# An explicit table for the side work of a Mamba and mixture-of-experts kernel

## The chip, the cores and the metric

The kernel runs on one core of a Trainium2 chip. The metric is device time in microseconds (us) of one launch, the median of several runs. Lower is better.

## The reference

The input `x` is 8 sequences of 512 tokens with 512 features, float32. Per sequence:

```
xz = W_in x ; x, z = halves (1024 channels each)
u  = silu(causal 4-tap convolution of x)
dt, B, C = W_x u (32 + 16 + 16 columns) ; delta = softplus(W_dt dt + b)
h_t = h_{t-1} * exp(delta_t * A) + delta_t * B_t * u_t      (1024 channels x 16 states)
y_t = sum over states of h_t * C_t, + D * u_t, times silu(z_t)
x1 = layernorm(x + W_out y)
out = layernorm(x1 + sum over the top 2 of 8 experts of weight * (E x1 + bias))
```

## The kernel before

**Main work.** Channels stand in 8 blocks of 128 partitions, and there are 16 states, so the recurrence of a sequence is 16 x 8 = 128 tiles of 128 x 512. The source calls each a row, numbered 0 to 127: row r is state r // 8 of block r % 8. Every row takes:

- ScalarE (ACT): `dA = exp(delta * A)`, L1384, into one of two PSUM buffers, so it waits for the scan two rows back;
- GpSimd (POOL): `dbu = u * B`, L1479, into one of four buffers, so it waits for the scan four rows back;
- VectorE (DVE): the scan `hst <- dA, dbu`, L1683.

Every second row TensorE (PE) transposes one block of 128 time steps of a finished state (8 transposes, L1053, called a part below) into `hTp`, and DVE adds it to `y` with weight C (L1511), one even row later. The sums of the last state of a sequence fall into rows 2 to 8 of the next one. SyncE (SP) issues nearly all DMAs, in one queue; at every eighth row it loads the next state's row of B, after the `dbu` of the row before.

**Side work.** All else is cut into pieces that are put between the rows of the main work, engine by engine. A piece has a name and a number, and on each engine where it has work it stands behind one row. An engine works through its rows in order: first the row's main instruction, then the row's pieces, each with its own semaphore waits. A piece whose wait is not over holds up all that stands behind it on that engine. While sequence b is scanned, the pieces do the experts' last four tiles and the output of b-2, the output projection, first layernorm, routing and experts of b-1, and the input projection, convolution and delta of b+1. Names that the text uses:

- `sz`: SP loads half a tile of silu(z) into `spare`; `gy`: POOL multiplies it into y (L1458); `yT`: PE transposes it, ACT copies it; `out`: PE multiplies by W_out (L1039, 8 shares), which `load_Wo` loads in two DMAs of 1 MB into `delta`;
- `load_res`, `load_hx`: SP loads the residual (4 DMAs) and the next sequence (1 MB, `hidT`);
- `xsL`, `moeL` (experts of tiles 11 to 14 of b-2) and `xsT`, `moe` (tiles 0 to 10 of b-1): PE transposes a tile of sorted tokens in `zs` (L1087) and multiplies by its expert's matrix (4 shares, L1039). The SP piece `xsL.k` waits until tile k is transposed and then loads tile k+2; the SP piece `moe.k` loads a later expert (1 MB) and stores the result;
- `x`: input projection, copied by ACT (L1261), three taps on DVE (L1540); `sig`, `sig2`: its silu on ACT (L1272 to L1279) and POOL (L1438); `scale`, `scatter`: ACT scales routed tokens, POOL scatters them (L1417);
- `skip`, `yinit` (PE L1071, ACT L1286), `dt`, `dt2`: D * u and delta of the next sequence; POOL ends each `dt` with two products (L1464, L1467);
- `fin`, `gather0`, `gather1`, `est`, `ln2`, `store`: the end of b-2.

**What sets the order.** `plan` (from L131 on) is a list scheduler in Python: it plays the five engines forward in steps of 0.1 us with the costs, waits and delays that `tasks` writes down for each piece, and takes, per engine, the most urgent piece that may start. `by_urgency` sorts the pieces by the length of the chain behind them plus a constant per group. `Segment` turns the result into `rows[engine][row]`, and derives from PE's order which PSUM bank and which half of `hTp` each piece uses. There are six segments: `SEG_FIRST` (head, no scan), `SEG_PRO` (sequence 0), `SEG_TWO` (1), `SEG_FULL` (2 to 6, the same table five times), `SEG_EPI` (7, whose rows are half tiles, 256 of them, scanned at L1691) and `SEG_LAST` (tail, no scan).

POOL's loop, shortened, shows how a piece stands behind a row:

```python
for step, pieces in w.rows("pool"):
    ...
    pool.wait_ge(scan_done, w.b * (NS * ND) + (n * ND + j - 3))
    nc.gpsimd.tensor_tensor(dbu[j % 4][:, :], u[w.odd][:, j, :], Bbc[n % 2][:, :], ALU.mult).then_inc(dbu_done, 1)
    ...
    for x in pieces:
        piece(w, x)
```

Of the kernel before, what the change touches and what calls it, by code (L numbers as in the profile page):

```python
# [49 lines left out]
def each(name, n):  # L50
    return [(name, j) for j in range(n)]


def per_tile(*names):
    return [(name, t) for t in range(NT) for name in names]


END = [x for g in range(0, NT, 2) for name in ("fin", "gather0", "gather1", "est", "ln2", "store") for x in ((name, g), (name, g + 1))]
MIX = [("load_Wo",)] + each("load_res", NT) + [x for t in range(NT) for x in (("sz", 2 * t), ("sz", 2 * t + 1), ("gy", 2 * t), ("gy", 2 * t + 1),
                                                                             ("yT", 2 * t), ("yT", 2 * t + 1), ("out", t))] \  # L60
    + per_tile("ln1") + each("x1T", NT) + [("gate",), ("count",), ("place",), ("route",)] + each("scale", TOP * NT) + each("scatter", TOP * NT)
def tokens(*tiles):
    return [x for k in tiles + (None,) for x in [("xsT", k)] * (k is not None) + [("moe", k - 1 if k is not None else tiles[-1])] * (k != tiles[0])]


LATE = TILES - 4
ROUTED = [("load_E",), ("load_T",), ("wT",)] + each("bias", NT) + [("load_E2",)]
MOE, MOE_EARLY = ROUTED + tokens(*range(TILES)), ROUTED + tokens(*range(LATE))
MOE_LATE = [({"xsT": "xsL", "moe": "moeL"}[x[0]], x[1]) for x in tokens(*range(LATE, TILES))]
Z = [x for i in range(HALF * NT) for x in (("z", i), ("z2", i))]  # L70
ZB = [x for i in range(HALF * NT) for x in (("zb", i), ("zb2", i))]
PRO = [("load_hx",), ("load_Wx",)] + each("x", ND) + [x for j in range(ND) for x in (("sig", j), ("sig2", j))] + [("load_wx",), ("xproj",), ("Ct",)] + each("skip", ND) + each("yinit", ND) + [x for j in range(ND) for x in (("dt", j), ("dt2", j))]


def den_tasks(x, mm):

    if x[0] != "den":
        return []
    t, e = LAST_DEN[x[1]]
    of_tile = [i for i, (u, _) in enumerate(LAST_DEN) if u == t and i < x[1]]  # L80
    late = [(("x1T", t), "act", 0.1), (("logits", NT - 1), "pe", 0)] if t >= PAIR else []
    return [("pe", mm, late + [(("load_D", e), "sp", 8 + 4 * e)] * (e in GONE)), ("dve", 0.7, [(x, "pe", 0.1), (("route", 1 if t >= PAIR else 0), "dve", 0)] + [(("den", i), "dve", 0) for i in of_tile[-1:]])]
# [7 lines left out]
def tasks(x, alone):  # L90


    name, k = x[0], x[-1] if len(x) > 1 else 0
    t = k // HALF if name in ("yT", "gy", "sz") else None
    mm, turn = 0.88, 0.6
    ev = "dve" if alone else "act"

    def silu(name, before_pe, before_act):

        if x[0] != name:  # L100
            return []
# [1645 lines left out]
```

## Time and profile before

| | |
|---|---|
| median of 3 runs | 2356.74 us (2356.3 to 2357.43) |
| profiled execution | 2358.6 us, first to last instruction |
| head, before the first scan | 72.9 us |
| sequence 0, 1, 2 | 240.6, 264.5, 277.2 us |
| sequences 3 to 6 | 272.6, 272.3, 273.9, 272.7 us |
| sequence 7 | 285.8 us |
| tail, after the last scan | 126.1 us |
| busy | DVE 89%, PE 89%, POOL 76%, ACT 64% |

The span is the only time that the profile gives for its execution; it is 1.9 us over the median of the runs. Sequence b begins with the start of its first scan: 578.0, 855.2, 1127.8, 1400.1 and 1674.0 us for b = 2 to 6. A row of the trace that gives idle time names in brackets how long the engine stood still before the instruction, and what ended that.

### The profile page before, as it was taken

What the parts mean: (1) busy time and instruction counts of PE and PEld (TensorE: products, weight loads), DVE (VectorE), ACT (ScalarE), POOL (GpSimd) and SP (SyncE); (2) the same over time, 40 slices, a digit from 0 to 9 for tenths busy, and PEclk for the clock granted to TensorE, in tenths of its full rate; (3) what the DMA queues carried; (4) which work ended last, traced back from release to release, by engine and by line L of the source; (5) the groups of instructions that cost most, each with busy time, mean ns of one, the idle gap of its engine ahead of it and who ended that gap; (6) DMA issues with size and microseconds to landing.
All of it is one profiled execution on the core that took longest, in us unless ns stands there. A gap on an engine that the chain in (4) does not pass through costs nothing.

```text
span 2358.6 us, 30155 instructions
## 1 busy us (share of the span) xinstructions
PE 2107.4 (89%) x8604; PEld 1220.5 (52%) x8604; DVE 2105.3 (89%) x2376; ACT 1516.0 (64%) x2742; POOL 1802.3 (76%) x1448
## 2 busy tenths in 40 slices
PE   9896779897989989899898998889898998889998
PEld 3344555555555555545554555455555455555543
DVE  5799999999999899999999999999999997899832
ACT  5747855785577666778566774778566785565411
POOL 2959996788887888879887889878888796685402
PEclk8896789898998999999999999999999998779999
DMA  5312031357544574446752576445743467475523
GB/s 172 108 34 74 19 139 50 128 177 258 152 109 143 179 274 132 126 148 223 255 126 93 174 266 210 112 148 201 268 125 108 154 224 255 113 246 176 185 75 84
DMA packets 205314, 367.93 MB, mean 156 GB/s; under 512 B 28472, under 2 KB 34744, under 8 KB 205152
## 3 DMA queue, kind: packets, MB, share of 16 engines
q1 hardware_dynamic: 190496, 335.60, 42.4%
q0 software_dynamic: 12544, 29.37, 5.8%
q8 instruction: 71, 1.16, 0.2%
q10 hardware_dynamic: 2112, 1.05, 0.2%
q14 instruction: 91, 0.75, 0.1%
HBM read 287.05 MB, written 78.91 MB: 155 GB/s over the span
## 4 chain that ended last, share of the span: by engine, by line
PE 29%; DVE 25%; POOL 24%; issue 12%; DMA 5%; ACT 4%; SPq 1%; DVEq 0%; POOLq 0%; ACTq 0%
PE bank L1039 20%; POOL dbu L1479 14%; DVE hst L1683 10%; DVE y L1511 6%; PE hTp L1053 6%; DVE hst L1691 3%; POOL u L1467 3%; DVE u L1540 2%; POOL delta L1464 2%; DMA zs<-sorted_tokens 2%; DMA ysb<-sorted_results,place 1%; POOL dbu L1487 1%; POOL sorted_tokens L1417 1%; ACT dA L1384 1%; PE bank L1172 1%
## 5 line engine op out<-in xcount | busy, mean ns | idle before, releaser
L1479 POOL TENSOR_TENSOR dbu<-u,Bbc 128x512 f32<-128x512 f32 x896 | 1144.6, 1313 | 210.2 <-DVE hst L1683 202.5
L1683 DVE TENSOR_TENSOR_SCAN hst<-dA,dbu 128x512 f32<-128x512 f32 x896 | 1051.8, 1205 | 17.8 <-ACT dA L1384 13.3
L1384 ACT ACTIVATE dA<-delta,negA 128x512 f32<-128x512 f32 (+1 forms) x1152 | 723.1, 639 | 457.7 <-DVE hst L1683 367.0
L1511 DVE SCALAR_TENSOR_TENSOR y<-hTp,Ct,y 128x1024 f32<-128x1024 f32 x512 | 646.2, 1262 | 47.3 <-PE hTp L1053 47.1
L1053 PEld LDWEIGHTS hTp<-ident,hst 128*128 128x128 f32 x4096 | 504.3, 151 | 354.2 <-issue 145.4
L1053 PE MATMUL hTp<-ident,hst 128*128 128x128 f32 x4096 | 574.9, 293 | 125.3 <-DVE hst L1683 34.7
L1039 PE MATMUL bank<-wslot,hidT 128*128 128x512 f32 x512 | 246.1, 616 | 21.9 <-ACT zs L1328 15.2
L1039 PE MATMUL bank<-delta,tokT 128*128 128x512 f32 x480 | 224.6, 604 | 1.5 <-issue 0.8
L1487 POOL TENSOR_TENSOR dbu<-u,Bbc 128x512 f32<-128x512 f32 x128 | 163.0, 1307 | 81.9 <-DVE hst L1691 65.4
L1039 PE MATMUL bank<-wslot,tokT 128*128 128x512 f32 x464 | 219.9, 604 | 2.6 <-ACT tokT L1343 2.1
L1039 PE MATMUL bank<-hidT,wslot 128*128 128x512 f32 x384 | 189.9, 640 | 10.0 <-DVE u L1540 7.7
L1540 DVE SCALAR_TENSOR_TENSOR u<-bank,cw,u 128x511 f32<-128x511 f32 (+2 forms) x192 | 142.1, 743 | 35.2 <-ACT u L1261 30.6
L1039 PEld LDWEIGHTS bank<-wslot,hidT 128*128 128x128 f32 x512 | 93.5, 196 | 114.5 <-issue 91.1
L1432 POOL DMA_INDIRECT ysb<-sorted_results,place x52 | 81.4, 1565 | 86.1 <-DMA ysb<-x_scratch 76.8
L1039 PEld LDWEIGHTS bank<-delta,tokT 128*128 128x128 f32 x480 | 87.3, 196 | 81.4 <-issue 79.8
L1039 PEld LDWEIGHTS bank<-wslot,tokT 128*128 128x128 f32 x464 | 82.3, 192 | 88.5 <-issue 79.4
L1039 PEld LDWEIGHTS bank<-hidT,wslot 128*128 128x128 f32 x384 | 74.3, 206 | 96.7 <-issue 77.5
L1438 POOL TENSOR_TENSOR u<-u,side 128x512 f32<-128x512 f32 x64 | 81.5, 1273 | 53.7 <-ACT side L1279 53.5
L1467 POOL TENSOR_TENSOR u<-delta,u 128x512 f32<-128x512 f32 x64 | 81.7, 1277 | 22.8 <-DVE delta L1557 17.4
L1446 POOL TENSOR_TENSOR zs<-zs,side 128x512 f32<-128x512 f32 x64 | 87.9, 1373 | 11.1 <-ACT side L1335 11.1
L1039 PE MATMUL bank<-wslot,side 128*128 128x512 f32 x192 | 94.2, 621 | 0.7 <-ACT side L1337 0.7
L1371 ACT ACTIVATE ysb<-bank 128x512 f32<-128x512 f32 x105 | 61.6, 587 | 49.9 <-PE bank L1039 41.5
(149 smaller groups left out, 2498.5 us busy)
## 6 DMA issues: line engine op xcount, KB each, us to landing
wslot<-in_w_expT SPq DMA_DIRECT2D x85, 1024.0 KB, 6.2
Bbc<-b_scratch SPq DMA_DIRECT2D x113, 256.0 KB
zs<-sorted_tokens SPq DMA_DIRECT2D x105, 256.0 KB, 3.1
sorted_results<-ysb SPq DMA_DIRECT2D x105, 256.0 KB, 6.0
wslot<-in_w_inT SPq DMA_DIRECT2D x26, 1024.0 KB, 5.4
res<-in_w_expT SPq DMA_DIRECT2D x18, 1024.0 KB, 5.7
gate_scratch<-zs SPq DMA_DIRECT2D x64, 256.0 KB, 2.1
delta<-in_w_outT SPq DMA_DIRECT2D x14, 1024.0 KB, 10.3
```

Source lines behind the costliest of these rows:

```text
L1039: mm = nc.tensor.matmul(dst, lhs(k), rhs(k), start=(k == 0), stop=(k == n - 1))
L1053: mm = nc.tensor.transpose(hTp[q % 2][:, tok(j)], hst[n % 2][:, j, start:start + P], ident[:, :])
L1384: nc.scalar.activation(decay_of(step, halved), delta[w.odd][:, j, cols], ACT.Exp, scale=negA[:, j, n:n + 1]).then_inc(exp_done, 1)
L1432: nc.gpsimd.indirect_dma_start(rows_of(w, t), None, ys_dram[:, :], bass.IndirectOffsetOnAxis(ap=place[:, w.odd, t, c:c + 1], axis=0), comp ...
L1438: nc.gpsimd.tensor_tensor(x_j, x_j, side[j % 2][:, :], ALU.mult).then_inc(x_ready, 1)
L1446: nc.gpsimd.tensor_tensor(zs[i % 2][:, :], zs[i % 2][:, :], side[i % 2][:, :], ALU.mult).then_inc(z_ready, 1)
L1467: nc.gpsimd.tensor_tensor(x_j, d, x_j, ALU.mult).then_inc(u_ready, 1)
L1479: nc.gpsimd.tensor_tensor(dbu[j % 4][:, :], u[w.odd][:, j, :], Bbc[n % 2][:, :], ALU.mult).then_inc(dbu_done, 1)
L1487: nc.gpsimd.tensor_tensor(dbu[k % 4][:, :].rearrange("p (k t) -> p k t", k=2), u[w.odd][:, j:j + 2, cols], Bbc[n % 2][:, cols].unsqueeze(1 ...
L1511: nc.vector.scalar_tensor_tensor(y_part, hTp[q % 2][:, :], Ct[odd][:, t, n:n + 1], y_part, ALU.mult, ALU.add).then_inc(acc_done, 1)
L1540: tap = nc.vector.scalar_tensor_tensor(late, bank[s][:, 0:L - k], cw[:, j, TAPS - 1 - k:TAPS - k], late, ALU.mult, ALU.add)
L1683: nc.vector.tensor_tensor_scan(hst[n % 2][:, j, :], dA[j % 2][:, :], dbu[j % 4][:, :], 0.0, ALU.mult, ALU.add).then_inc(scan_done, 1)
```

## The change

`tasks`, `plan`, `by_urgency`, their cost tables and the groups of pieces go. In their place stands a table per segment and engine, `ORDER_FIRST` to `ORDER_LAST`: text of the form `row: piece piece | row: piece`, where `*4` on PE is a number of shares. `parse` reads it, and `Segment` derives rows, banks and halves from it as before. The engines' loops and pieces are the same.

```diff
-def plan(pieces, steps, pace):
...
+def parse(text, shares):
+
+    rows = []
+    for entry in text.split(" | ") if text else []:
+        row, work = entry.split(": ")
+        for word in work.split():
+            piece, _, times = word.partition("*")
+            name, *number = piece.split(".")
+            rows += [(int(row), (name,) + tuple(int(k) for k in number))] * (int(times or 1) if shares else 1)
+    return rows
...
+ORDER_FULL = {
...
+    "pool": "5: gy.0 | 12: gy.1 | 19: gy.2 | 23: gy.3 | 25: gy.4 | 26: gy.5 | 32: gy.6 | 33: gy.7 | 37: gather0.0 | 40: gather0.1 | 41: gather1.0 | 42: gather1.1 | "
...
```

Head and tail keep every piece in its place. In the other segments single pieces stand a few rows from where the planner put them. In `SEG_FULL`, the five-fold one, the moves that the text speaks of are:

| engine | piece | row before | row now |
|---|---|---|---|
| POOL | gy.0, gy.1, gy.2 | 7, 9, 17 | 5, 12, 19 |
| POOL | scatter.0; sig.1 | 76; 75 | 75; 76 |
| POOL | sig.2 | 79, behind scatter.6 and .7 | 78, ahead of them |
| POOL | dt.2, dt.4 | 103, 111 | 108, 113 |
| POOL, DVE | gather1.2; est.2 | 55; 55 | 53; 53 |
| SP | xsL.11, load_Wo, load_hx | 0, in the order load_Wo, load_res, load_hx, xsL.11 | 0, 0, 2, in the order xsL.11, three load_res, load_Wo, load_res, xsL.12, load_hx |
| PE | xsL.13 | 12 | 10 |
| PE | yinit.3 | 104 | 106 |
| PE | xproj, 8 shares | 84 and 86 | 84 |
| PE | moe.1 to moe.3 | row 102 holds five shares of moe.2 and .3 | spread over 96 to 102, one share in 102 |
| ACT | yinit.2 | 107, behind dt.4 | 106, ahead of dt.4 |

**POOL at the start of a full sequence.** `spare` is the tile that `sz` loads, L1479 is the main product of a row (L1318 in the changed file), L1458 the piece `gy` (L1297). Before, from the product of row 7 on:

```order
L1479 TENSOR_TENSOR dbu3<-u0,Bbc0 128x512
L1458 TENSOR_TENSOR y1<-y1,spare0 128x512
L1479 TENSOR_TENSOR dbu0<-u0,Bbc1 128x512
L1479 TENSOR_TENSOR dbu1<-u0,Bbc1 128x512
L1458 TENSOR_TENSOR y1<-y1,spare1 128x512
```

and now, from the product of row 4 on:

```order
L1318 TENSOR_TENSOR dbu0<-u0,Bbc0 128x512
L1318 TENSOR_TENSOR dbu1<-u0,Bbc0 128x512
L1297 TENSOR_TENSOR y1<-y1,spare0 128x512
L1318 TENSOR_TENSOR dbu2<-u0,Bbc0 128x512
L1318 TENSOR_TENSOR dbu3<-u0,Bbc0 128x512
L1318 TENSOR_TENSOR dbu0<-u0,Bbc1 128x512
```

The first `gy` now stands ahead of the products of rows 6 and 7.

**SP's queue at the same place.** Before:

```order
L809 DMA Bbc1<-b_scratch 128x512
L873 DMA spare0<-gate_scratch 128x512
L873 DMA spare1<-gate_scratch 128x512
L819 DMA delta1<-in_w_outT 128x4x512 x2
L860 DMA res<-in_hid 128x512 x4
L913 DMA hidT<-in_hidT 128x4x512
L823 DMA zs1<-sorted_tokens 128x512
L823 DMA zs0<-sorted_tokens 128x512
```

and now:

```order
L648 DMA Bbc1<-b_scratch 128x512
L712 DMA spare0<-gate_scratch 128x512
L712 DMA spare1<-gate_scratch 128x512
L662 DMA zs1<-sorted_tokens 128x512
L699 DMA res<-in_hid 128x512 x3
L658 DMA delta1<-in_w_outT 128x4x512 x2
L699 DMA res<-in_hid 128x512
L662 DMA zs0<-sorted_tokens 128x512
L752 DMA hidT<-in_hidT 128x4x512
```

The load of token tile 13 (`zs1`) passed 3 MB of other loads; the two loads of `spare` kept their place, and what is ahead of them is the same.

**PE around rows 102 to 108.** `hst` are the main transposes of a part, `side` those of `yinit`, `wslot` and `res` hold experts. Before:

```order
L1039 MATMUL bank<-wslot,tokT 128x512 x4
L1087 MATMUL hTp<-ident,zs 128x128 x8
L1140 MATMUL bank<-rows,w_rows 128x512
L1053 MATMUL hTp<-ident,hst 128x128 x8
L1071 MATMUL hTp<-ident,side 128x128 x8
L1039 MATMUL bank<-wslot,tokT 128x512 x4
L1053 MATMUL hTp<-ident,hst 128x128 x16
```

and now:

```order
L878 MATMUL bank<-wslot,tokT 128x512
L926 MATMUL hTp<-ident,zs 128x128 x4
L979 MATMUL bank<-rows,w_rows 128x512
L926 MATMUL hTp<-ident,zs 128x128 x4
L892 MATMUL hTp<-ident,hst 128x128 x8
L910 MATMUL hTp<-ident,side 128x128 x4
L878 MATMUL bank<-wslot,tokT 128x512 x4
L892 MATMUL hTp<-ident,hst 128x128 x8
L878 MATMUL bank<-res,tokT 128x512
L910 MATMUL hTp<-ident,side 128x128 x4
L892 MATMUL hTp<-ident,hst 128x128 x8
```

Three shares went ahead of this stretch, and one `yinit` behind the part of row 106.

## Rows read from the trace of the kernel before

**Rows 1.** The page: busy time of the engines.
```profile
PE 2107.4 (89%) x8604; PEld 1220.5 (52%) x8604; DVE 2105.3 (89%) x2376; ACT 1516.0 (64%) x2742; POOL 1802.3 (76%) x1448
```
**Rows 2.** Windows: sequences 2 and 4; the first line names the columns.
```profile
core 0: us, PE busy (x) PEld busy (x) DVE busy (x) ACT busy (x) POOL busy (x), PEclk, DMA share, GB/s
578.00:855.20 277.20, 256.45 (x1062) 148.20 (x1061) 256.84 (x275) 189.07 (x332) 228.85 (x184) 0.92 0.51 160
...
1127.80:1400.10 272.30, 248.05 (x1070) 144.30 (x1069) 255.80 (x274) 188.97 (x333) 228.71 (x184) 0.96 0.55 177
```
**Rows 3.** DVE's waits, rows 9 to 17 of sequences 3, then 6: us, times, longest.
```profile
DVE y L1511 <- PE hTp L1053: 1.4, 2, 1.1
DVE hst L1683 <- ACT dA L1384: 0.7, 1, 0.7
...
DVE hst L1683 <- ACT dA L1384: 2.3, 1, 2.3
DVE y L1511 <- PE hTp L1053: 1.1, 2, 0.8
```
**Rows 4.** PE's timeline in sequence 4, from row 12 on: start, us, instruction, idle before.
```profile
1151.87 1.08 PE L1087 MATMUL hTp<-ident,zs 128*128 128x128 f32 x4 [4.38 <-DMA zs<-sorted_tokens]
```
**Rows 5.** Windows of sequence 4 around that wait, and 19 us later.
```profile
1149.00:1165.00 16.00, 12.11 (x49) 8.49 (x50) 12.88 (x13) 6.32 (x12) 13.39 (x11) 0.68 0.83 307
1168.00:1184.00 16.00, 15.98 (x76) 9.77 (x75) 15.82 (x17) 10.02 (x20) 14.26 (x12) 1.00 0.64 198
```
**Rows 6.** PE's and DVE's timelines in sequence 4, rows 104 to 108.
```profile
1358.65 3.60 PE L1039 MATMUL bank<-wslot,tokT 128*128 128x512 f32 x8
1362.56 1.94 PE L1053 MATMUL hTp<-ident,hst 128*128 128x128 f32 x16 [0.31 <-ACT y L1286]
...
1363.67 1.28 DVE L1511 SCALAR_TENSOR_TENSOR y<-hTp,Ct,y 128x1024 f32<-128x1024 f32 x1 [1.60 <-PE hTp L1053]
```
**Rows 7.** Windows of sequence 4: rows 83 to 107.
```profile
1313.00:1363.00 50.00, 49.24 (x219) 27.30 (x218) 48.03 (x45) 39.17 (x67) 43.66 (x36) 1.00 0.55 185
```
**Rows 8.** Timelines of sequence 4, rows 77 to 79: ACT, DVE.
```profile
1301.26 0.63 ACT L1272 ACTIVATE side<-u 128x512 f32<-128x512 f32 x1 [2.00 <-POOL u L1438]
...
1304.52 1.53 DVE L1540 SCALAR_TENSOR_TENSOR u<-bank,cw,u 128x511 f32<-128x511 f32 x2 [0.96 <-ACT u L1261]
```
**Rows 9.** POOL's timeline in the same rows.
```profile
1298.94 0.98 POOL L1417 DMA_INDIRECT sorted_tokens<-zs,place  x1 [0.30 <-issue]
1299.95 1.27 POOL L1438 TENSOR_TENSOR u<-u,side 128x512 f32<-128x512 f32 x1
```
**Rows 10.** POOL's timeline, the first gy of sequences 3, 4, 5, 6.
```profile
867.05 1.26 POOL L1458 TENSOR_TENSOR y<-y,spare 128x512 f32<-128x512 f32 x1 [4.07 <-DMA spare<-gate_scratch]
868.27 1.28 POOL L1479 TENSOR_TENSOR dbu<-u,Bbc 128x512 f32<-128x512 f32 x1
1139.11 1.26 POOL L1458 TENSOR_TENSOR y<-y,spare 128x512 f32<-128x512 f32 x1 [3.54 <-DMA spare<-gate_scratch]
1412.55 1.27 POOL L1458 TENSOR_TENSOR y<-y,spare 128x512 f32<-128x512 f32 x1 [4.63 <-DMA spare<-gate_scratch]
1685.02 1.27 POOL L1458 TENSOR_TENSOR y<-y,spare 128x512 f32<-128x512 f32 x1 [3.25 <-DMA spare<-gate_scratch]
```
**Rows 11.** SP's timeline, start of sequence 4: when it issued what.
```profile
1130.49 0.40 SPq L815 DMA_DIRECT2D wslot<-in_w_expT  x1
...
1132.38 1.35 SPq L873 DMA_DIRECT2D spare<-gate_scratch  x2
```
**Rows 12.** DVE's timeline, the scan of row 6 in sequences 3, 4, 5, 6.
```profile
865.96 1.21 DVE L1683 TENSOR_TENSOR_SCAN hst<-dA,dbu 128x512 f32<-128x512 f32 x1
...
1138.56 2.33 DVE L1683 TENSOR_TENSOR_SCAN hst<-dA,dbu 128x512 f32<-128x512 f32 x2
...
1410.91 1.21 DVE L1683 TENSOR_TENSOR_SCAN hst<-dA,dbu 128x512 f32<-128x512 f32 x1
...
1684.76 2.32 DVE L1683 TENSOR_TENSOR_SCAN hst<-dA,dbu 128x512 f32<-128x512 f32 x2
```

More of the change, by code:

```diff
@@ L47 @@
 ENGINES = ("sp", "pe", "act", "pool", "dve")
[L50 to L61, printed above, removed]
@@ L62, in tokens @@
-def tokens(*tiles):
-    return [x for k in tiles + (None,) for x in [("xsT", k)] * (k is not None) + [("moe", k - 1 if k is not None else tiles[-1])] * (k != tiles[0])]
-LATE = TILES - 4
[L67 to L82, printed above, removed]
+LATE = TILES - 4
@@ new lines, with __init__ @@
+class Segment:
+    def __init__(self, order, blocks, next_blocks, steps=STEPS):
+        placed = {engine: parse(order[engine], engine == "pe") for engine in ENGINES}
+        begun = {}
+        for row, x in placed["pe"]:
+            begun.setdefault(x, row)
+        users, turns = [], [x for x in begun if x[0] in TURNED]
+        for x in begun:
+            if x[0] in LOGITS:
+                users += [(LOGITS[x[0]], x[1] // PAIR)] * (x[1] % PAIR == 0)
+            elif x[0] not in TURNED:
+                users.append(x)
@@ L338, in __init__ @@
         self.turned = {x: k for k, x in enumerate(turns)}
-        self.turned_at = {x: row for row, x, _ in order["pe"] if x[0] in TURNED}
+        self.turned_at = {x: begun[x] for x in turns}
         self.half = {x: sum(self.turned_at[y] == self.turned_at[x] for y in turns[:k]) for x, k in self.turned.items()}
@@ L347, in __init__ @@
         self.after = {x: (self.blocks[s] + next_blocks[s:s + 1])[k + 1:k + 2] for x, (s, k) in self.place.items()}
-        self.rows = {engine: [[(x, share) if engine == "pe" else x for row, x, share in order[engine] if row == k] for k in range(steps or 1)] for engine in ENGINES}
+        self.rows = {engine: [[] for _ in range(steps or 1)] for engine in ENGINES}
+        for engine in ENGINES:
+            shares = {}
+            for row, x in placed[engine]:
+                shares[x] = shares.get(x, -1) + 1
+                self.rows[engine][row].append((x, shares[x]) if engine == "pe" else x)
 W_Z = [[("Wz", 0)], [("Wz", 1)]]
@@ L386, in by_urgency @@
-def by_urgency(bonus):
-    pieces = [x for g in bonus for x in GROUPS[g]]
-    work = {}
-    for x in pieces:
-        for e, cost, after in tasks(x, False):
-            shares = SHARES.get(x[0], 1) if e == "pe" else 1
-            work[x, e] = cost * shares * (1.5 if shares > 1 else 1), after
-    then = {key: [((x[0], x[1] + 1), e, 0) for x, e in [key] if len(x) > 1 and ((x[0], x[1] + 1), e) in work] for key in work}
-    then = {key: [((x, e), delay) for x, e, delay in after] for key, after in then.items()}
-    for key, (_, after) in work.items():
-        for y, e, delay in after:
-            if (y, e) in then:
-                then[y, e].append((key, delay))
-    rest = {}
-    def tail(key):
-        if key not in rest:
-            rest[key] = work[key][0] + max([delay + tail(k) for k, delay in then[key]], default=0)
-        return rest[key]
-    group = {x: g for g in bonus for x in GROUPS[g]}
-    return sorted(pieces, key=lambda x: -max([tail((x, e)) for e in ENGINES if (x, e) in work], default=0) - bonus[group[x]])
@@ L417 @@
[L417 to L420 removed]
+ORDER_FIRST = {
[5 rows of a table added]
+}
```

258 lines of the change are left out of this document (17 added, 241 removed), and 106 rows, old and new, of tables (ORDER_EPI, ORDER_FIRST, ORDER_FULL, ORDER_LAST).

## Prediction

> **What bounds the kernel now.** I read the page's busy shares first. PE and DVE are busy for 89% of the span each, 2107.4 and 2105.3 us [rows 1]; no engine is saturated, so waits set the time. Then I read one window per sequence. A scanning sequence takes DVE at least its busy time: 256.84 of 277.20 us in sequence 2, 255.80 of 272.30 in sequence 4 [rows 2]. DVE does the scans, which the whole program follows, so the 20.4 and 16.5 us it stands idle there are all that moving pieces can win in such a sequence. PE's busy time in them, 256.45 and 248.05 us, is nearly as long, so part of that idle time may not be winnable. The change removes no instruction. I therefore priced each move by the DVE wait it takes away or adds. Five such sequences share one table, so a microsecond there counts up to five times.
>
> **A: token tile 13 comes earlier (gain).** In rows 14 to 17, DVE stands still for a `dA` and for a part's transposes: 0.7 + 1.4 us in sequence 3, and 2.3 + 1.1 in sequence 6 [rows 3]. The four sequences 3 to 6 have this pair, in all 11.1 us (5.6 for `dA`, 5.5 for `y`); sequence 2 has not. Its source stands in PE's timeline: PE waits 4.38 us for the DMA into `zs` [rows 4], and the 16 us around it run at a granted clock of 0.68, PE busy 12.11 us; 19 us later 16 us run at 1.00, PE busy 15.98 [rows 5]. That load was issued behind W_out, the residual and the next sequence (3 MB), and is now issued ahead of them; PE's `xsL.13` moves from row 12 to 10, but the 3 MB are worth more than two rows (5 us at the 307 GB/s of that window would move 1.5 MB). I take the whole 11.1 us. Bounds: 0 (something else is late there) and 11.1.
>
> The clock reached its lower level (1.2 GHz in part of that window) after PE's standstill. The Trainium skill ("TensorE: Matmul & The Clock Gate", section "HAM oscillation — how this bites in real kernels") says that a standstill of the array is what brings the clock down, and that the slow spell outlasts it. By that rule the new stall under E could starve PE and lower the clock anew; the `y` waits of A, 5.5 us of the 11.1, would then return and the sum below would be −6.5 instead of −12.0. By the row alone nothing says that a stall of POOL reaches PE so early, so the sum takes A whole.
>
> **B: `yinit.3` behind the part of row 106, `yinit.2` ahead of `dt.4` on ACT (gain).** DVE waits 1.60 us for the part of row 106, whose transposes PE began after 8 shares and a wait of 0.31 us for ACT [rows 6]. It does so in each of the five, 8.0 us, plus 2.0 us for the `dA` behind it. The moved `yinit` is 8 of the 16 side transposes, some 0.5 us, and the wait for ACT goes: 0.31. Together 0.8 to 1.0 us of each wait, so 5 of 10 us. More isn't there, for PE was busy 49.24 of the 50 us before [rows 7]: three shares of row 102 moved earlier stay in the same saturated stretch. Bounds 0 and 10.
>
> **C: `sig.2` ahead of two scatters on POOL (gain).** Row 78's taps wait 0.96 us for ACT's copy into `u`; ACT had waited 2.00 us for POOL's product [rows 8]. That product stood behind two scatters and starts at 1299.95, the second scatter at 1298.94 [rows 9]: ahead of them it is done 1 to 2 us sooner. The wait of 0.9 to 1.0 us stands in all five: gain 4.6. Bounds 0 and 4.6.
>
> **E: the first `gy` at row 5 instead of 7 (loss).** In sequences 3 to 6 POOL's `gy.0` waits for `spare`, 3.25 to 4.63 us, and starts at 867.05, 1139.11, 1412.55 and 1685.02 [rows 10]. It starts when the tile lands, not when POOL gets there. What precedes that load in SP's queue is as before: an expert (1 MB) issued at 1130.49, the two `spare` halves at 1132.38 [rows 11]. So `gy.0` still starts then, but the `dbu` of rows 6 and 7 now stand behind it. Row 6's `dbu` ends 1.26 + 1.28 us after each start: 869.6, 1141.7, 1415.1, 1687.6. Its scan started at 865.96, 1138.56, 1410.91 and 1684.76 [rows 12]. DVE loses 3.6, 3.1, 4.2 and 2.8 us, in all 13.7. What was covered by four `dbu` buffers (POOL could run ahead of the scans while it waited) loses that cover. ACT and PE stand behind DVE there and only gain room. Bounds: 0 (the tile lands as early as POOL gets there) and 13.7. I take 13.7, as four sequences show nearly the same landing.
>
> **The rest: a gain of 5 us.** Sequences 0, 1 and 7 have moves of the same kind, and the five full ones have small ones: `gather1.2` and `est.2` two rows up, 0.3 us or nothing, since DVE there waits for the gather; `xproj` gathered in row 84; POOL's `dt` pieces later. Sequence 2 has idle time that sequence 4 has not, 3.9 us [rows 2]. I take 5 us in all, most of it from that. Bounds: a loss of 15 (each of seven sequences 2 us worse) and a gain of 10. Head and tail keep their places: nothing.
>
> **Sum.** −11.1 − 5.0 − 4.6 + 13.7 − 5.0 = −12.0 us. The profiled execution took 2358.6 us, so 2346.6; the median of the runs is 1.9 us lower than that execution, and the forecast on its basis is 2356.7 − 12.1 = 2344.6 us. Adding only the gain ends of the bounds gives −36 (about 2321), only the loss ends +29; both need every term at one end.
>
> **The rivals.**
>
> 1. *The first `gy` does not stall.* With tile 13 and the order of loads changed the sequences shift, and the `spare` halves may land before POOL reaches row 5. Against it: four starts fall 3.25 to 4.63 us after POOL was ready two rows later [rows 10]. For it: sequence 2 shows no such wait, and the expert load ahead waits for PE to give up a slot, which could now come earlier. Then E is 0 and the sum is −25.7: 2331 us. In the trace loads land in the order in which they were issued: `spare`, issued at 1132.38, by 1139.11, and `zs`, issued after it, by 1151.87 [rows 4, 10]. The Trainium skill ("DMA: Bandwidth & Descriptors", section "Queues, rings and completion order") says that descriptors of one queue start in order but several engines work side by side, with nothing ordering them among each other. By it `spare` need not wait for the whole expert load, which speaks for this rival; the rows show no case of it. Chance 0.24.
>
> 2. *Waits form again.* PE has 24 us of slack per full sequence in sequence 4, but none in rows 83 to 107 [rows 7]. What DVE gains earlier, it may lose there, since PE's work up to row 107 isn't less. B then gives nothing, and A and C come back as longer waits at row 107 and behind: E's 13.7 us stand against the little that is left. 2357 us, within the 0.2% (4.7 us) that a measurement of this kernel can tell from no change. Chance 0.15.
>
> 3. *POOL becomes the bound, slower.* POOL is busy 228.7 of 272.3 us [rows 2]. `dt.2` moves from row 103 to 108, where it stands just ahead of the next one: two `dt` pieces of two products each, 1.3 us a product, among rows that need a `dbu` every 2 us. Four buffers hold what POOL is ahead; having lost 3 us at row 6 and doing `sig.2` and the scatters late, it may not be ahead. One `dt` not covered is 2.6 us of DVE idle in each of five sequences: 13. With B and C lost to it: −11.1 − 5 + 13.7 + 13 = +10.6, so 2367 us. It decides from the point where each full sequence loses 2.4 us more than in my sum. Against it: in the trace DVE waits for no `dbu` behind the `dt` pieces. Chance 0.15.
>
> **How the numbers follow.** The forecast, A to E as summed, with B, C and the rest each some us off, has 0.46 and its own range of 2336 to 2351 us. Rival 1 has 0.24 (2324 to 2336), rival 2 0.15, rival 3 0.15 (to 2374). The range takes in the first three and the nearer part of the third: 2324 to 2362, leaving about 0.1 at either side together with what I haven't thought of. Faster by over 0.2% (under 2352.0) are the forecast and rival 1: 0.70. Same: 0.15. Slower: 0.15.
>
> **What would show it.** Right: sequences 3 to 6 without PE's 4 us wait for `zs` and with a granted clock near 1 in rows 10 to 17; no `dA` wait at row 14; a wait of DVE for `dbu` of about 3 us at row 6, and POOL's `gy.0` still starting when `spare` lands; the wait at row 107 near 0.7 us; row 78 without a wait; full sequences of about 270 us. Wrong: `gy.0` starting at once behind the product of row 5 (rival 1); unchanged sums of DVE's idle time with PE as the cause, moved to rows 107 to 121 (rival 2); `hst <- POOL dbu` in the rows behind 77 or 108 (rival 3). The forecast is wrong as a whole if the full sequences take less than 266 or more than 272 us.

## The result, and the profile after

| | before | changed |
|---|---|---|
| median | 2356.52 us (2354.91 to 2357.43, 4 runs) | 2392.85 us (2380.49 to 2397.15, 4 runs) |
| profiled execution | 2358.6 us | 2390.7 us |

The change is slower: the ratio is 1.0131, with a 95% interval of 1.0099 to 1.0163. The forecast was 2344.6 us with a range of 2324 to 2362; the result lies above it; "slower" had a chance of 0.15. In every run the time is 1.8 us more than the span, so the profile before, of 2358.6 us, belongs to an execution of about 2360.4 us, 4 us above the median: the two profiles differ by 32.1 us, the medians by 36.3.

The page's busy times show that no work was added. PE's 14.7 us more than in [rows 1] are the same 8604 matmuls, mostly at a lower clock (0.919 granted over the span, 0.923 before); DVE's 6.3 us are treated below:

```profile
PE 2122.1 (89%) x8604; PEld 1229.7 (51%) x8604; DVE 2111.6 (88%) x2376; ACT 1510.7 (63%) x2742; POOL 1801.7 (75%) x1448
```

Windows of the changed kernel, one per sequence (2 to 7), same columns as [rows 2]:

```profile
580.72:856.84 276.12, 252.24 (x1062) 146.04 (x1061) 257.84 (x274) 187.85 (x332) 227.84 (x184) 0.94 0.53 165
856.84:1136.75 279.91, 253.52 (x1070) 146.17 (x1069) 258.30 (x274) 188.61 (x334) 229.52 (x185) 0.95 0.55 172
1136.75:1420.70 283.95, 256.44 (x1070) 150.60 (x1069) 257.81 (x274) 189.01 (x334) 229.60 (x185) 0.93 0.54 170
1420.70:1697.52 276.82, 249.66 (x1070) 146.65 (x1069) 258.13 (x274) 188.24 (x334) 229.66 (x185) 0.96 0.56 174
1697.52:1973.57 276.05, 248.90 (x1070) 143.86 (x1069) 257.85 (x275) 188.45 (x334) 229.48 (x185) 0.96 0.56 175
1973.57:2262.85 289.28, 245.66 (x1054) 154.84 (x1053) 259.82 (x405) 160.65 (x373) 193.07 (x154) 0.87 0.60 188
```

Sequence 2 is 1.0 us shorter than before, 3 is 7.3 longer, 4 is 11.6, 5 is 3.0, 6 is 3.4, 7 is 3.5. One table gives five different results, so its cost is no fixed amount per sequence.

**The ledger.** I read the start of every scan from both traces and added up the time from row to row over sequences 2 to 6 (us; all else in the last column but one). The stretches end at rows where few pieces cross. This is arithmetic on scan starts, each line from one profiled execution, and every run below is read by the same columns:

| profile of | rows 0-7 | 8-23 | 24-41 | 42-55 | 56-73 | 74-95 | 96-127 | rest | span |
|---|---|---|---|---|---|---|---|---|---|
| before | 71.5 | 160.2 | 175.7 | 150.5 | 240.7 | 274.7 | 295.4 | 989.9 | 2358.6 |
| changed | 85.0 | 150.3 | 175.4 | 142.9 | 250.9 | 293.0 | 295.4 | 997.8 | 2390.7 |
| difference | +13.5 | -9.9 | -0.3 | -7.6 | +10.2 | +18.3 | 0.0 | +7.9 | +32.1 |

What was forecast for rows 0 to 23 came. The loss was made in rows 56 to 95, and in "rest" (sequences 0, 1, 7 and the tail: +1.2, +1.4, +3.5, +1.7).

**Rows 0 to 7, term E.** POOL's and DVE's timelines in sequence 3:

```profile
868.63 1.26 POOL L1297 TENSOR_TENSOR y<-y,spare 128x512 f32<-128x512 f32 x1 [6.97 <-DMA spare<-gate_scratch]
869.85 7.41 POOL L1318 TENSOR_TENSOR dbu<-u,Bbc 128x512 f32<-128x512 f32 x6
```
```profile
871.20 2.45 DVE L1522 TENSOR_TENSOR_SCAN hst<-dA,dbu 128x512 f32<-128x512 f32 x2 [3.47 <-issue]
```

POOL stands 6.97 us for `spare` ([rows 10]: 4.07, two products later), and the scan of row 6 starts 3.47 us late, 0.1 us behind the end of its `dbu`. The profile puts this wait to "issue"; the product that ends with it tells whose it is.

**Rows 69 to 73, not in the forecast at all.** POOL's and DVE's timelines in sequence 3; the short DVE instructions are the routing piece `place` of row 71:

```profile
1002.86 1.27 POOL L1285 TENSOR_TENSOR zs<-zs,side 128x512 f32<-128x512 f32 x1 [4.99 <-ACT side L1174]
1004.09 3.72 POOL L1318 TENSOR_TENSOR dbu<-u,Bbc 128x512 f32<-128x512 f32 x3
```
```profile
1004.24 0.19 DVE L1462 TENSOR_REDUCE tiles<-over 128x8 f32<-128x32 f32 x1
1004.46 0.93 DVE L1464 TENSOR_TENSOR_SCAN end<-ones,tiles 128x8 f32<-128x8 f32 x1
1005.42 1.19 DVE L1466 TENSOR_TENSOR begin<-end,tiles 128x8 f32<-128x8 f32 x1
1006.53 1.41 DVE L1467 TENSOR_TENSOR past<-ramp,end 1x120 f32<-1x120 f32 x1
1007.87 0.17 DVE L1470 SCALAR_TENSOR_TENSOR row<-begin,bank 128x32 f32<-128x32 f32 x1
```

The same three instructions before:

```profile
1003.54 0.17 DVE L1625 TENSOR_TENSOR_SCAN end<-ones,tiles 128x8 f32<-128x8 f32 x1
1003.75 0.17 DVE L1627 TENSOR_TENSOR begin<-end,tiles 128x8 f32<-128x8 f32 x1
1003.84 0.26 DVE L1628 TENSOR_TENSOR past<-ramp,end 1x120 f32<-1x120 f32 x1
```

Two things happen. First, POOL's piece `z.7` stands 4.99 us for ACT's `z2.7`: this ACT piece moved from row 69 to row 72, behind `x.1`, which itself waits for PE, while POOL's `z.7` moved up from row 73 to 72, behind `sig.0`. In sequences 4 and 5 the wait is 7.9 us. Second, POOL then makes up for it with three products in a row, 1.24 us each from 1004.09 on, and three of DVE's instructions on tiny tiles last until one of them ends: 1005.39, 1006.61 and 1007.94 against product ends of 1005.36, 1006.59 and 1007.81. The 32 short instructions of this piece and its neighbours take 7.6 us per sequence before and 9.1 after; some met a product before, too, for in e12 below they take 5.4 to 6.0. All of DVE's busy time in rows 56 to 73, over sequences 2 to 6, grew from 223.1 to 231.0 us and its idle time from 17.6 to 19.8: most of the +10.2 is instructions that took longer, not waits.

The Trainium skill ("SBUF — State Buffer", section "SBUF: two separate sides") says that VectorE and GpSimd share one pair of ports, which one instruction holds to its end, against VectorE instructions with two SBUF inputs among others. The ends in these rows agree with it to 0.15 us: the three that lasted have two SBUF inputs, and `tiles`, with one, took 0.19 us while the first of the products ran.

**Rows 80 to 87.** Windows of sequence 3, rows 74 to 79 and 80 to 87, before and then changed:

```profile
1013.82:1036.20 22.38, 18.83 (x66) 8.96 (x64) 21.13 (x25) 19.29 (x32) 19.45 (x17) 1.00 0.55 180
1036.20:1052.27 16.07, 15.29 (x58) 8.34 (x59) 16.07 (x17) 9.05 (x16) 12.39 (x11) 0.89 0.61 219
```
```profile
1016.36:1038.79 22.43, 17.70 (x60) 8.21 (x58) 21.11 (x25) 17.96 (x30) 20.13 (x18) 0.97 0.36 124
1038.79:1062.34 23.55, 23.55 (x71) 11.88 (x70) 16.49 (x18) 11.02 (x19) 13.96 (x12) 0.66 0.51 164
```

In the last window PE has no idle time at all (23.55 of 23.55 us) and a granted clock of 0.66, so most of it ran at 1.2 instead of 2.4 GHz; DVE was busy for only 16.49 us. PE's timeline just before and in it:

```profile
1033.34 1.04 PE L1006 MATMUL bank<-ident,wt 128*8 128x128 f32 x8 [1.19 <-DVE u L1379]
1035.57 0.63 PE L926 MATMUL hTp<-ident,zs 128*128 128x128 f32 x4 [1.18 <-DMA zs<-sorted_tokens]
1037.36 1.80 PE L1011 MATMUL bank<-w_rows,rows 8*128 8x512 f32 x2 [1.17 <-ACT rows L1213]
...
1045.74 3.78 PE L1011 MATMUL bank<-w_rows,rows 8*128 8x512 f32 x4
```

Three waits of 1.2 us, and then four bias matmuls take 3.78 us that took 1.98 in the same place before:

```profile
1040.50 1.98 PE L1172 MATMUL bank<-w_rows,rows 8*128 8x512 f32 x4
```

DVE's longest wait is that of row 87 for the part of row 86. Before, PE did four shares of `xproj` (8 matmuls), a part, and the other four:

```profile
1043.44 3.65 PE L1039 MATMUL bank<-u,hidT 128*64 128x512 f32 x8
1047.01 1.09 PE L1053 MATMUL hTp<-ident,hst 128*128 128x128 f32 x8
1048.04 3.65 PE L1039 MATMUL bank<-u,hidT 128*64 128x512 f32 x8
```

Now the part of row 86 stands behind all eight shares:

```profile
1051.35 8.72 PE L878 MATMUL bank<-u,hidT 128*64 128x512 f32 x16
1060.00 1.10 PE L892 MATMUL hTp<-ident,hst 128*128 128x128 f32 x8
```
```profile
1061.14 1.28 DVE L1350 SCALAR_TENSOR_TENSOR y<-hTp,Ct,y 128x1024 f32<-128x1024 f32 x1 [4.02 <-PE hTp L892]
```

Over sequences 2 to 6, DVE waits for PE's parts in rows 74 to 95 for 5.0 us before and 22.9 in the change, most of it at rows 87 and 91. This is what sets the two orders apart in all 17 profiles of this document: 4.0 to 6.4 us in the nine with the old order of these rows, 12.9 to 22.9 in the eight with the new one.

The kernel before has the slow spell of the clock too, but in its profile only in sequence 2 (19.7 us at 0.61):

```profile
758.67:778.41 19.74, 19.74 (x51) 9.39 (x50) 16.59 (x18) 8.68 (x14) 12.79 (x11) 0.61 0.51 186
```

Sequence 2's rows 72 to 95 took 69.6 us, the others' 61.8 to 62.6. That covers the 3.9 us more of idle time in sequence 2, which the forecast had taken for something the table could mend.

### The profile page after: what moved, and what is told of

It reads as the page before. It is cut to its first block, busy times and chain, and to the rows that moved or that the text cites. A ratio compares the mean times of both kernels' runs of the same rounds, so it can differ in the third digit from the quotient of the medians.

```text
span 2390.7 us, 30155 instructions
## 1 busy us (share of the span) xinstructions
PE 2122.1 (89%) x8604; PEld 1229.7 (51%) x8604; DVE 2111.6 (88%) x2376; ACT 1510.7 (63%) x2742; POOL 1801.7 (75%) x1448
## 4 chain that ended last, share of the span: by engine, by line
PE 45%; DVE 19%; POOL 17%; issue 9%; ACT 5%; DMA 3%; SPq 0%; DVEq 0%; POOLq 0%; ACTq 0%
PE bank L878 28%; PE hTp L892 10%; POOL dbu L1318 9%; DVE hst L1522 7%; DVE y L1350 5%; DVE hst L1530 3%; PE bank L979 2%; DVE u L1379 2%; POOL u L1277 2%; PE bank L1011 1%; PE hTp L926 1%; POOL sorted_tokens L1256 1%; ACT dA L1223 1%; POOL dbu L1326 1%; DMA spare<-gate_scratch 1%
## 5 line engine op out<-in xcount | busy, mean ns | idle before, releaser
L1318 POOL TENSOR_TENSOR dbu<-u,Bbc 128x512 f32<-128x512 f32 x896 | 1147.2, 1330 | 183.2 <-DVE hst L1522 178.4
L892 PE MATMUL hTp<-ident,hst 128*128 128x128 f32 x4096 | 592.2, 297 | 158.6 <-ACT tokT L1180 36.3
L892 PEld LDWEIGHTS hTp<-ident,hst 128*128 128x128 f32 x4096 | 517.8, 154 | 401.0 <-issue 207.4
L1100 ACT ACTIVATE u<-bank,cb,cw 128x512 f32<-128x512 f32 x64 | 49.2, 769 | 75.0 <-PE bank L878 75.0
```

Source lines behind the costliest of these rows:

```text
L892: mm = nc.tensor.transpose(hTp[q % 2][:, tok(j)], hst[n % 2][:, j, start:start + P], ident[:, :])
```

## The experiments

The tables make single moves easy to undo. I first wrote the planner's order as tables too; a stretch of rows of `ORDER_FULL` could then be taken from either. Every run has its own interval against the kernel before on the same chip. Medians of before were 2361.55 us in the first four runs, 2359.14 in the next four, 2357.95 in the third and 2360.59 in the last three; single executions scatter more there (2349 to 2371) than in the runs of the result. A profile shows one execution and not the median: that of e12 had 2345.9 us where the median is 2357.2, that of e5 2357.7 where it is 2367.8. Where two runs of different groups are compared by their medians, the ratios can give some us more or less.

### Which table, which rows

**e1**, the changed kernel with the old `ORDER_FULL`:

> The changed kernel with the old order in the table of sequences 2 to 6 alone; sequences 0, 1 and 7, head and tail stay as changed. Theory 1 (the loss is made inside the five full sequences, +24 us there by the two traces, and +1.2, +1.4, +3.5 and +1.7 us in sequences 0, 1, 7 and the tail): about 2364 us, against 2392.9 for the change. Theory 2 (the new orders of sequences 0 and 1 hand a late state on, which the full ones repeat): over 2375.

Measured: 2367.61 us, ratio 1.0031 (1.0008 to 1.0054). Theory 1 holds for the sum: the other tables cost about 7 us (2 to 13 by the interval), the full one the rest. Of these 7 us its profile shows only 3 in "rest"; rows 74 to 95, with the old table, took 283.8 us, with slow spells in three sequences.

```diff
-    "pe": "2: xsL.11 xsL.12 | 6: moeL.11*4 moeL.12 yT.0 | 8: moeL.12 | "
+    "pe": "2: xsL.11 xsL.12 | 6: moeL.11*4 yT.0 moeL.12*2 | 10: moeL.12 | "
...
```

**e2**, rows 0 to 41 of `ORDER_FULL` old, the rest as changed:

> The changed kernel with the old order in rows 0 to 41 of sequences 2 to 6, the new one from row 42 on and everywhere else. Theory 1 (stages are independent: row 6 loses 13.6 us, rows 9 to 24 give 9.7 back, the main loss is made behind row 56): about 2389 us. Theory 2 (the loss behind row 56 follows from the stall at row 6, by the time at which PE and its clock come there): 2365 us or less.

```diff
-    "pool": "5: gy.0 | 12: gy.1 | 19: gy.2 | "
+    "pool": "7: gy.0 | 9: gy.1 | 17: gy.2 | "
...
```

Measured: 2369.56 us, ratio 1.0033 (1.0014 to 1.0052), 18 us below the change (2387.73 in its own repeat). Rows 0 to 23 explain none of it: 71.0 + 161.4 here, 85.9 + 147.3 in the change's second profile. So theory 1, 2389 us, is wrong. But the mechanism of theory 2 isn't shown either: without the stall, rows 56 to 95 still take 250.5 + 285.6 = 536.1 us, against 515.4 before and 543.9 and 541.8 in the two profiles of the change. Most of the loss behind row 56 needs no stall at row 6.

**e3**, the kernel before with the new rows 0 to 41:

> The kernel before with the new order in rows 0 to 41 of sequences 2 to 6 alone. Theory 1: about 2360.5 us (+13.6 at row 6, -9.7 in rows 9 to 24), with a wait of about 3 us of DVE at row 6 of sequences 3 to 6 and rows 56 to 127 timed as before. Theory 2: 2380 us or more, and half-clock stretches in rows 80 to 91.

```diff
-    "pool": "7: gy.0 | 9: gy.1 | 17: gy.2 | "
+    "pool": "5: gy.0 | 12: gy.1 | 19: gy.2 | "
...
```

Measured: 2369.85 us, ratio 1.0031 (1.0010 to 1.0052), +7 us by the ratio. Rows 0 to 7 take 85.2 us and rows 8 to 23 take 150.5, just as theory 1 has it; but rows 80 to 87 fell into the slow spell in sequences 4, 5 and 6 (clock 0.62 to 0.63), with an unchanged table there. The time lies between the theories (2360.5 and 2380 us).

### gy.0

**e4**, one piece moved back in the changed kernel:

> The changed kernel with POOL's first gy back from row 5 to row 7 in sequences 2 to 6, nothing else. Theory 1: the 13.6 us of waits at row 6 go and nothing takes their place: about 2379 us. Theory 2 (DVE meets PE's work later instead): over 2387 us.

```diff
-    "pool": "5: gy.0 | 12: gy.1 | "
+    "pool": "7: gy.0 | 12: gy.1 | "
...
```

**c**, the changed kernel again:

> The changed kernel once more, so that the experiments have it on their own chip. Theory 1 (its time is the sum of its parts: 2365.3 us with gy at row 7, and 13.7 us of waits at row 6): about 2379 us. Theory 2 (the stall at row 6 also pushes sequences into the half-clock spell in rows 80 to 91): 2385 to 2393 us, and over 5 us more than 2379.

**e5**, the opposite of e4, on the kernel before:

> The kernel before with POOL's first gy at row 5 instead of 7 in sequences 2 to 6, nothing else. Theory 1 (each stall at row 6 lengthens its sequence by its own length): +13.7 us against the kernel before, 2375 us where that takes 2361.6. Theory 2 (the late PE pieces of rows 12 to 17 now hide behind the stall, so part comes back there): +5 us or less.

```diff
-    "pool": "7: gy.0 | 9: gy.1 | "
+    "pool": "5: gy.0 | 9: gy.1 | "
...
```

**e6**, e3 with `gy.0` at row 7:

> The kernel before with the new order in rows 0 to 41 of sequences 2 to 6, but gy.0 left at row 7. Theory 1 (the earlier load of token tile 13 gives back 9.7 us in rows 9 to 24 and nothing else changes): 2352 us where the kernel before takes 2361.6. Theory 2 (the gain moves the sequences into another half-clock spell or returns as waits behind row 56): within 3 us of the kernel before.

| run | median us | ratio to before | rows 0-7 | 8-23 | 56-73 | 74-95 | rest |
|---|---|---|---|---|---|---|---|
| c | 2387.73 | 1.0122 (1.0101 to 1.0144) | 85.9 | 147.3 | 258.5 | 283.3 | 995.8 |
| e4 | 2365.30 | 1.0012 (0.9993 to 1.0030) | 72.2 | 148.8 | 249.0 | 293.0 | 988.9 |
| e5 | 2367.81 | 1.0027 (1.0007 to 1.0047) | 83.2 | 146.0 | 243.8 | 271.7 | 990.0 |
| e6 | 2352.86 | 0.9977 (0.9953 to 1.0000) | 70.7 | 153.7 | 237.8 | 278.2 | 988.8 |

The stall at row 6 is the move of `gy.0`: rows 0 to 7 take 83 to 88 us in every profile that has it at row 5, and 71 to 74 in every one that has it at row 7. With it back, the change is 22 us faster by the medians and 26 by the ratios, where e4's own theories had about 2379 us and over 2387 us; 22 is 8 to 9 us more than the stall itself. That is theory 2 of c by its time, but not by its mechanism: rows 74 to 95 took 283.3 us in c and 293.0 in e4. What c has on top of the stall in its profile stands in rows 56 to 73 (9.5 us) and in "rest" (6.9), whose tables are the same.

In e5 the same stall costs 6 us by the ratio (9 by the medians), near theory 2 and half of theory 1. The columns, of an execution in which it cost nothing (2357.7 us), show how it can be less: rows 8 to 23 fall from 160.2 to 146.0 us although the loads stand in their old order. While DVE waits at row 6, PE and the DMA of tile 13 catch up (PE's 4 us wait for `zs` is gone in three of four sequences, 2.0 us in the other), and DVE's waits of [rows 3] are gone. Terms A and E are thus two ways to spend the same waits; the change has moved the loads and put in the stall, and so is paid once. e6, the loads without the stall, gains 5 us by the ratio (0 to 11), between its theories.

### Rows 42 to 73, and z2.7

**e7**, four POOL products back, on the changed kernel:

> The changed kernel with four POOL products (z.5, z.6, z.7, sig.0) back in rows 67, 71, 73, 73 of sequences 2 to 6. Theory 1 (DVE's short routing instructions of rows 69 to 72, 0.2 us each, take 1.2 us when they meet a POOL product; in the changed trace they sum to 9.1 us per sequence, before to 7.6): they fall back to about 7.6 us and rows 64 to 72 to about 22.5 us, 7 us or more off the whole. Theory 2 (rows 64 to 72 are longer because of PE's order): no change beyond 3 us.

```diff
-           "69: z.5 | 70: z.6 | 72: sig.0 z.7 | "
+           "67: z.5 | 71: z.6 | 73: z.7 sig.0 | "
```

Measured: 2378.60 us, ratio 1.0084 (1.0059 to 1.0110), 9 us below c. The size is theory 1's, the mechanism isn't: the short DVE instructions still take 8.4 to 8.7 us a sequence, and POOL's wait at `z.7` is 6.2 to 9.5 us long. In the profile the difference lies in rows 74 to 95 (275.8 us, all but one sequence without a slow spell there) and in rows 56 to 73 (252.3).

**e8**, the kernel before with the new rows 0 to 55 and `gy.0` at row 7:

> The kernel before with the new order in rows 0 to 55 of sequences 2 to 6 and gy.0 at row 7: run e6 (2352.9 us beside 2359.1) plus the new order of rows 42 to 55, where the earlier gather takes DVE's wait for it from 2.3 to 0.8 us. Theory 1 (these 1.5 us per sequence stay): e6 less 7 us, about 14 us below the kernel before. Theory 2 (they come back behind row 56): as e6.

Measured: 2343.71 us, ratio 0.9940 (0.9919 to 0.9960). Rows 42 to 55 take 143.1 us instead of 150.5, and this stays: 142 to 143 us in every profile with the new order there, 150 to 151 in every one with the old. Theory 1.

**e9**, rows 56 to 73 old:

> The changed kernel with the old order in rows 56 to 73 of sequences 2 to 6. Theory 1 (rows 56 to 73 lose about 4 us per sequence, since POOL's z.7 waits 5 to 8 us for ACT's z2.7, moved behind x.1): 2368 us where the change takes 2387.7. Theory 2 (the clock in rows 80 to 91 decides): the gain depends on the sequences hit there, under 10 us on the mean.

**e10**, rows 74 to 110 old:

> The changed kernel with the old order in rows 74 to 110 of sequences 2 to 6. Theory 1 (the loss in rows 72 to 96 is a half-clock spell that the old order has too, only less often, and rows 102 to 107 gave 0.5 us each): 2380 to 2388 us, with some sequences at 62 us for rows 72 to 95 and others at 66 to 70. Theory 2 (the new PE order of rows 74 to 91 is itself slower): 2375 us or less.

**e11**, a single ACT piece back:

> The changed kernel with one ACT piece, z2.7, back from row 72 to row 69 in sequences 2 to 6. Theory 1 (POOL's z.7 no longer stands 5 to 8 us, its products no longer fall upon DVE's routing instructions of row 71): POOL's wait under 3 us, DVE's short instructions back to about 7.5 us a sequence, 7 us or more off the changed kernel, about 2378. Theory 2 (four buffers cover POOL's stall and the collisions fall elsewhere): within 4 us of it.

```diff
-           "69: z.7 | 71: sig.0 sig2.0 gate x.1 | 72: z2.7 | "
+           "69: z.7 z2.7 | 71: sig.0 sig2.0 gate x.1 | "
```

**e13**, the opposite of e11, on the kernel before:

> The kernel before with ACT's z2.7 moved from row 69 to 72 in sequences 2 to 6, nothing else. Theory 1 (the move is costly by itself: POOL waits at z.7 behind ACT's x.1, then runs its late products into DVE's routing instructions): +10 us or more against the kernel before, and short DVE instructions of over 8.5 us a sequence. Theory 2 (costly only with POOL's z.7 moved ahead to row 72): within 4 us of the kernel before.

```diff
-           "69: z.7 z2.7 | 71: sig.0 sig2.0 gate x.1 | "
+           "69: z.7 | 71: sig.0 sig2.0 gate x.1 | 72: z2.7 | "
```

| run | median us | ratio to before | rows 56-73 | 74-95 | short DVE instructions, us a sequence |
|---|---|---|---|---|---|
| c | 2387.73 | 1.0122 (1.0101 to 1.0144) | 258.5 | 283.3 | 8.7 to 9.7 |
| e9 | 2373.80 | 1.0076 (1.0049 to 1.0103) | 241.7 | 290.2 | 6.2 to 6.6 |
| e10 | 2378.62 | 1.0084 (1.0051 to 1.0117) | 256.2 | 275.5 | 9.8 to 11.1 |
| e11 | 2364.31 | 1.0016 (0.9995 to 1.0038) | 238.9 | 279.0 | 5.5 to 8.5 |
| e13 | 2370.13 | 1.0052 (1.0031 to 1.0074) | 245.5 | 279.3 | 9.3 to 10.2 |

Moving one ACT piece of two activations back takes 23 of the 29 us off that the change loses on these chips, where theory 1 asked for 7 or more. DVE's busy time in rows 56 to 73 falls with it, from 231.0 us (c) to 218.8; in e13 it rises from 223.1 to 232.3, so the single move does in both directions what the change did there. Put into the kernel before alone, it costs 12 us by the ratio, 10 by the medians (theory 1). POOL's timeline of e11 in sequence 3, at the place of the 4.99 us wait above:

```profile
996.75 2.50 POOL L1294 TENSOR_TENSOR dbu<-u,Bbc 128x512 f32<-128x512 f32 x2 [2.45 <-DVE hst L1498]
1006.62 1.03 POOL L1232 DMA_INDIRECT sorted_tokens<-tokT,place  x1 [7.37 <-ACT tokT L1174]
```

The wait at `z.7` is gone from these rows; what POOL waits for is a scan, and then the first tokens to scatter. In sequences 4 and 6 no short DVE instruction lasts longer than 0.5 us. In e9, whose rows 56 to 73 are old, the 10 us of the ledger there are gone (241.7 us), but rows 74 to 95 stay long, as the new order of these rows is still in; its 14 us by the medians lie between its theories.

e10 was worth 9 us by the medians, where theory 2 asked for 12 or more: near the border between them. Over all profiles rows 74 to 95 tell it better: with the old order they took 274.7, 283.8, 281.4, 271.7, 278.2, 266.7, 275.5, 279.3 and 273.5 us, on the mean 276; with the new one 293.0, 283.3, 285.6, 293.0, 275.8, 290.2, 279.0 and 286.1, on the mean 286. The new order of these rows takes 10 us more, and either order scatters by 17 us. The pieces of all engines changed there, but it is DVE's wait for PE that rose (above): the eight shares of `xproj` in one row are the piece in front of its wait at row 87. No run moved `xproj` alone.

### Both back

**e12**, the changed kernel with `gy.0` at row 7 and `z2.7` at row 69:

> The changed kernel with both pieces back: gy.0 at row 7 and z2.7 at row 69. Theory 1 (independent losses of 22.4 and 23.4 us): 2387.7 - 45.8 = 2342 us, or 2345 with what is off. Theory 2 (they share a loss, as either alone already brought the change to 2365): 2355 to 2365 us.

Measured: 2357.20 us (2344.66 to 2372.27), ratio 0.9991 (0.9969 to 1.0012). With the two pieces moved, the change can't be told from the kernel before. The two losses are not independent (45.8 us would have been their sum, 30.5 it is): theory 2.

**e14**, new rows 0 to 73 with both pieces back, old rows 74 to 127, other sequences as before:

> The kernel before with the new order in rows 0 to 73 of sequences 2 to 6, but gy.0 at row 7 and z2.7 at row 69. Theory 1 (run e8, 2343.7 us beside 2358.0, and the 0.8 us per sequence by which rows 64 to 71 were shorter in run e11): 2340 us, the fastest of all. Theory 2 (the shorter rows 64 to 71 come back as a wait in rows 72 to 80): as e8.

Measured: 2341.73 us (2335.55 to 2347.22), ratio 0.9917 (0.9897 to 0.9937). This is 19 us below the kernel before and the lowest median of all, 2 us from the 2340 of theory 1; its interval overlaps that of e8, so that the two theories aren't told apart. Its windows of sequence 4, rows 80 to 87 and 88 to 95, show the stretch without a spell:

```profile
1298.13:1314.21 16.08, 15.30 (x58) 8.29 (x59) 16.08 (x18) 9.09 (x16) 12.40 (x11) 0.89 0.64 239
1314.21:1329.62 15.41, 15.41 (x75) 9.08 (x74) 14.13 (x14) 14.22 (x26) 12.23 (x11) 1.00 0.24 70
```

The same stretches of e12 in a good sequence (5), still the new order, take 1.1 us more, for DVE's waits of 0.7 and 1.3 us for PE at rows 87 and 91 remain when the clock does not fall:

```profile
1570.54:1587.62 17.08, 17.01 (x69) 9.30 (x68) 16.32 (x18) 10.84 (x19) 13.93 (x12) 0.90 0.69 229
1587.62:1603.17 15.55, 14.76 (x69) 8.36 (x69) 14.02 (x14) 13.02 (x23) 12.29 (x10) 1.00 0.47 142
```

What stays open: what decides whether rows 80 to 95 fall into the slow spell. In e6 the same table gives 60.6 us for rows 72 to 95 in one sequence and 69.5 in another. Over all profiles PE's waits of over 0.4 us in rows 70 to 86 sum to 3 to 8 us a sequence, with a spell or without. No run put work into these waits alone, so that they cause the spell is argued from the order in time, not shown. Open is also why the gains of the two pieces don't add.

## Why the prediction was wrong

By its own steps, with the ledger's columns:

- **What bounds the kernel.** That DVE's idle time is all that can be won was right as far as it goes. But every instruction was priced at a fixed length: DVE's busy time in rows 56 to 73 rose by 7.9 us, and PE's slack ("24 us" a sequence) is none in rows 80 to 87 once the clock falls, so that part of the idle time that I took for DVE's own was PE at 1.2 GHz.
- **A**, -11.1: measured -9.9 in rows 8 to 23. Right in place and nearly in size, in part by luck: of the waits it named, those for `dA` went from 5.6 to 0.5 us, those for `y` only from 5.5 to 3.7 (2.5 and 1.2 us at row 17 of sequences 4 and 6, at clocks of 0.78 and 0.82 in rows 10 to 17). The load passed 4 MB and not 3: W_out is 2 MB, the residual and the next sequence 1 MB each; the reading doesn't hang on it. And "nothing says that a stall of POOL reaches PE so early" was wrong: PE now stands 2.7 to 4.4 us at row 8 of sequences 3 to 6, and at most 1.2 with `gy.0` back (e4). What was missed above all is that the stall of E would have removed these waits alone (e5).
- **B**, -5.0: rows 96 to 127 show 0.0. The wait at row 107 fell from 1.60 to 1.22 us, as forecast in kind, but 0.45 us came up at row 105 and 0.39 us at row 117. Moving pieces where PE is saturated here only moved the wait, as rival 2 said.
- **C**, -4.6: the waits of row 78 sum to 2.8 us instead of 4.7, shorter in two of the five sequences and gone in one, which waits 1.5 us at row 76 instead. It drowned in rows 74 to 95, which lost 18.3 us.
- **E**, +13.7: measured +13.5, waits of 3.5, 2.9, 3.0 and 4.2 us. The method worked here: the time at which a tile lands, plus the products behind it, minus the start of the scan.
- **The rest**, -5.0: this is the step that failed. Its gains and losses were +10.2 (rows 56 to 73), +18.3 (74 to 95), -7.6 (42 to 55) and +7.9 (elsewhere), in sum +28.8. Even its bound of +15 was too small. Two pieces stand out. The ACT piece `z2.7` was not named at all: behind `x.1` it held POOL up and, through late products, stretched DVE's short instructions (e11, e13). "`xproj` gathered in row 84" was named and put at nothing without a reason: DVE's wait for PE at row 87 went from 0.6 to 11.8 us over the five sequences, 5 to 13 in every profile with the new order and at most 1.4 with the old (0.7 us in a sequence whose clock held, 4.0 in a spell). "DVE there waits for the gather", for which I took 0.3 us, was a real gain: rows 42 to 55 got 1.5 us shorter each time, and kept it (e8). And the 3.9 us of sequence 2 that I counted as winnable were a spell of low clock. How the +7.9 elsewhere splits between table and scatter stays open ("rest" was 987.8 to 996.8 us in the other profiles with these tables).
- **The rivals.** Rival 1 (no stall at `gy.0`) is excluded: POOL waited 6.4 to 7.7 us in all four sequences. Rival 3 (slower, through POOL) had the right side and the right engine, but its place was wrong: rows 96 to 127 lost nothing, so the `dt` pieces are innocent. POOL is late with products 35 rows earlier, and costs DVE busy time there, no wait for a `dbu`. Rival 2 (waits for PE form again) was nearest for rows 74 to 95, but stopped at what the gains were worth (2357 us).
- **The chance.** The bound of +15 for the rest came from "2 us per sequence". The spell alone made one sequence 7 us longer in the profile of before (69.6 against 61.8 to 62.6 us in rows 72 to 95). [rows 2] show the lower clock of that sequence, 0.92 against 0.96, and I did not use it as a bound.

## What to carry to other kernels

Price a moved piece by who waits for it on the other engines, not by its own length: a piece of two activations (1.3 us), put behind one that waits for PE, held POOL for 5 to 8 us, and with it everything queued there. Where two engines are busy for 90%, test moves one at a time on the chip and keep those that pay: the table lost 1.3% as a whole, and its rows 0 to 73 of the five full sequences, with two pieces back and all else left alone, gained 0.8%. And before counting an idle stretch as a reserve, look at the clock in it, and at whether another planned gain already spends the same wait.

## What was not expected of the hardware

- DVE instructions on tiles of 128 x 8 and 1 x 120 took 0.93 to 1.41 us instead of 0.17 to 0.26 when they met products of POOL, each until a product ended (rows above). Over the five full sequences this made 7 to 8 us more than before.
- The granted clock fell to 0.61 to 0.69 over rows 80 to 87 in one to three sequences of 11 of the 17 profiles, under both orders, and rows 72 to 95 of the same table then took 3 to 9 us more. PE's longest waits in rows 77 to 81, just ahead of it, were of 1.2 to 1.4 us in the new order and of 2 to 3 us in the old, and sequences that kept the clock had them too.
- Losses were not additive: taking back `gy.0` alone gave 22 us, `z2.7` alone 23 us, both 30.5 us.
